# Routing the last three batches through one expert a token, in a two-layer attention and mixture kernel

## The reference, cut to what matters

```python
probs = softmax(xt @ Wg)                       # 2048 tokens, 8 experts
sel   = top_k(probs.T, 256)                    # each expert picks 256 tokens
tok2exp = argmax over the experts that picked it, else over all
weights = probs[token, tok2exp]
for e in range(8):
    gate = where(tok2exp == e, weights, 0)
    out += gate * (gelu(xt @ W1[e]) @ W2[e])   # W1: 128x256, W2: 256x128
x = x + gb * out
```

## Time and profile before

| | us |
|---|---|
| median of 3 runs | 757.88 (756.86 to 758.79) |
| the profiled execution's span | 758.0 |
| PE busy | 738.9 (97%) |
| DVE busy | 550.8 (73%) |
| ACT busy | 383.1 (51%) |
| POOL busy | 187.3 (25%) |

### The profile page before, as it was taken

How to read it: one execution, slowest core, us unless ns; L and a number is a source line. 1 busy time by engine, 2 the same in 40 slices (tenths; PEclk the granted TensorE clock), 3 DMA queues, 4 the chain that set the end, 5 groups by cost and what they waited for, 6 DMA issues and landing times.

```text
span 758.0 us, 16817 instructions
## 1 busy us (share of the span) xinstructions
PE 738.9 (97%) x6559; PEld 558.0 (74%) x6559; DVE 550.8 (73%) x1642; ACT 383.1 (51%) x1063; POOL 187.3 (25%) x235
## 2 busy tenths in 40 slices
PE   7899999999999999999999999999999899999996
PEld 5666757775786578657865776688578778999996
DVE  4877785868867886778677867787959664255997
ACT  3755656355545654564456445643561446554422
POOL 0232522154015402530253025304210422000000
PEclk9999999999999999999999999999999999999999
DMA  7950020402040204020302130113204304000000
GB/s 229 397 120 1 29 57 2 112 1 57 8 106 2 57 19 96 2 56 20 96 2 55 28 87 18 41 39 76 57 2 113 112 3 111 1 1 1 16 21 22
DMA packets 55702, 43.07 MB, mean 57 GB/s; under 512 B 37900, under 2 KB 48804, under 8 KB 54216
## 3 DMA queue, kind: packets, MB, share of 16 engines
q1 hardware_dynamic: 55624, 42.01, 20.7%
HBM read 32.42 MB, written 9.58 MB: 55 GB/s over the span
## 4 chain that ended last, share of the span: by engine, by line
PE 85%; DVE 9%; ACT 2%; DMA 1%; issue 1%; POOL 1%; SPq 0%; DVEq 0%; ACTq 0%
PE ps L1755 15%; PE ps L1838 14%; PE ps L1898 8%; PE ps L2061 4%; PE ps L2039 4%; PE ps L1741 4%; PE ps L2008 4%; PE ps L1763 4%; PE ps L1850 3%; PE ps L1789 3%; PE ps L1776 3%; DVE shared L1484 2%; DVE shared L1477 2%; PE ps L1705 2%; PE ps L1921 2%; PE ps L1933 2%
## 5 line engine op out<-in xcount | busy, mean ns | idle before, releaser
L1755 PE MATMUL ps<-veF,hB 128*128 128x512 f32 x256 | 121.5, 606 | 0.0
L1303 DVE COPY_PREDICATED shared<-ghot,ps 128x512 f32<-128x512 int32 x128 | 88.2, 726 | 3.4 <-PE ps L1755 0.6
L850 ACT ACTIVATE sc<-sc,nmax 128x128 f32<-128x128 f32 (+1 forms) x128 | 57.2, 447 | 58.3 <-DVE nmax L1289 58.3
L1755 PEld LDWEIGHTS ps<-veF,hB 128*128 128x128 f32 x256 | 45.2, 189 | 49.4 <-issue 40.5
L650 POOL TENSOR_TENSOR sc<-sc,rg 128x384 f32<-128x384 f32 x64 | 51.6, 827 | 70.0 <-DVE rg L1276 70.0
L707 POOL TENSOR_TENSOR ve<-mv,eps 128x2 f32<-128x2 f32 x24 | 8.6, 357 | 229.9 <-DVE mv L1189 229.9
L1838 PE MATMUL ps<-early_masks,oeF 128*128 128x256 f32 x256 | 62.9, 385 | 0.0
L1838 PE MATMUL ps<-wide,oeF 128*128 128x256 f32 x256 | 62.3, 386 | 0.0
L1898 PE MATMUL ps<-hC,early 128*64 128x128 f32 x1024 | 61.7, 275 | 0.1
L2039 PE MATMUL ps<-hE,veF 128*128 128x256 f32 x256 | 59.5, 382 | 0.3 <-ACT wide L959 0.3
L1898 PEld LDWEIGHTS ps<-hC,early 128*64 128x64 f32 x1024 | 55.6, 137 | 5.3 <-issue 3.4
(11 more groups left out here) (253 smaller groups left out, 1529.5 us busy)
## 6 DMA issues: line engine op xcount, KB each, us to landing
chosen<-hot_scratch SPq DMA_DIRECT2D x16, 512.0 KB, 5.8
v_scratch<-shared SPq DMA_DIRECT2D x16, 512.0 KB, 5.2
vg<-v_scratch SPq DMA_DIRECT2D x16, 512.0 KB, 5.4
veF<-in_L_ffn_value_experts SPq DMA_DIRECT2D x1, 2048.0 KB, 9.3
oeF<-in_L_ffn_output_experts SPq DMA_DIRECT2D x1, 2048.0 KB, 14.2
early<-in_L_attn_w_qkv SPq DMA_DIRECT2D x1, 1536.0 KB, 14.9
shared<-bias_scratch SPq DMA_DIRECT2D x2, 512.0 KB, 5.8
veF<-in_L_ffn_W SPq DMA_DIRECT2D x1, 1024.0 KB, 5.2
```

Source lines behind the costliest of these rows:

```text
L850: act.activation(v, v, ACT.Exp, bias=nmax[:, h % RING, t:t + 1], scale=-1.0, accum_out=denB[:, h * T + t:h * T + t + 1]).then_inc(s_("f_e" ...
L1303: dve.copy_predicated(val[:, t, :].rearrange("p (h k) -> p h k", h=HF), ghot[:, t * HF:(t + 1) * HF, e].bitcast(I32).unsqueeze(2) .broadca ...
L1755: pe.matmul(ps[:, vbank(j), :], tok(hB, t), veF[:, :].rearrange("p (h e k) -> p e h k", h=HF, e=EF)[:, e, :, :], start=True, stop=True).th ...
```

## The change

Batches 0 to 4 stay dense (`DENSE = 5`). The 768 tokens of batches 5 to 7 (six tiles) are sorted by expert. Each expert's tokens fill whole tiles of 128 places, the rest of its last tile is padding, so 13 tiles (`PLACES = 6 + 8 - 1`) hold any split of them. A row has 386 numbers: the token's features, its x, its gate, its weight and its number.

- GpSimd prepares constants and the x, gate, number and weight parts of the rows; TensorE turns the features of the six tiles back in slots of batches 2 and 3, and ScalarE copies them into the rows. SP fills the scratch of 13 x 128 rows in DRAM with padding.
- VectorE chooses first for the six sorted tiles, then for the ten dense ones. TensorE counts with seven small matmuls in slot 28 of batch 4 how many tokens of the same expert stand ahead of each. VectorE works out each token's place and each tile's expert.
- GpSimd writes the rows to their places with six indirect DMAs, SP reads them back in five loads, GpSimd copies the W1 of each tile's expert to a fixed place (13 register loads, 13 copies of 128x256).
- TensorE does eight filling matmuls, loads 13 registers, and then in 17 steps transposes tile j, multiplies tile j-2 with its W1 and tile j-4 with its W2, with ScalarE's copy and GELU between.
- VectorE does the kept batches 0 to 3, sorted tiles 0 to 3, kept batch 4, sorted tiles 4 to 12. A sorted tile is two operations: output times weight times gate, and the sum with x. GpSimd stores each finished tile to its tokens' rows of the output with an indirect DMA; numbers beyond the last token (padding) are dropped.
- `direct_one`, `last_tile` and the dense work of batches 5 to 7 on TensorE and ScalarE are gone. Old semaphores are used a second time under new names (`since` adds the count reached before).

```diff
+DENSE = KEPT
+SORTED_B = B - DENSE
+SORTED_T = SORTED_B * T
+FIRST_T = DENSE * T
+PLACES = SORTED_T + E1 - 1
...
+LOADS = ((0, 1), (1, 2), (2, 5), (5, 10), (10, 13))
+FILL = 8
+TURNED_BACK = {(2, 2 * E1 + 6): (0, 2), (3, 2 * E1 + 6): (2, 3)}
+COUNTED_AT = (4, 28)
+WEIGHED = ()
...
+            since(sp, "t_ones", 4)
+            sp.dma_start(sorted_dram.rearrange("(j p) c -> p j c", p=P),
+                         padding.unsqueeze(1).broadcast_to([P, PLACES, ROW])).then_inc(s_("t_padded"), 16)
+
+            sp.wait_ge(s_("t_sorted"), 16 * SORTED_T)
+            for i, (lo, hi) in enumerate(LOADS):
+                sp.dma_start(rows_of(lo, hi), sorted_dram.rearrange("(j p) c -> p j c", p=P)[:, lo:hi, :]
+                             ).then_inc(s_("t_rows%d" % i), 16)
...
+            for i in range(SORTED_B):
+                b = DENSE + i
+                pool.tensor_copy(staged(i)[:, :, ID_AT].bitcast(I32), token_no[:, i * T:(i + 1) * T]).then_inc(s_("t_staged"), 1)
+                pool.tensor_copy(staged(i)[:, :, D:2 * D], x[:, b * T:(b + 1) * T, :]).then_inc(s_("t_staged"), 1)
+                pool.tensor_copy(staged(i)[:, :, 2 * D:3 * D],
+                                 gate1[:, b, :].unsqueeze(1).broadcast_to([P, T, D])).then_inc(s_("t_staged"), 1)
...
+            since(pool, "t_staged", 4 * SORTED_B)
+            since(pool, "t_h", SORTED_B)
+            since(pool, "t_padded", 16)
+            since(pool, "t_place", 1)
+            for i in range(SORTED_T):
+                pool.indirect_dma_start(sorted_dram, bass.IndirectOffsetOnAxis(ap=token_place[:, i:i + 1], axis=0),
+                                        staged(i // T)[:, i % T, :], None).then_inc(s_("t_sorted"), 16)
+
+            since(pool, "t_expert", 1)
+            for j in range(PLACES):
+                e = pool.value_load(expert_of[0:1, j:j + 1], min_val=0, max_val=E1 - 1)
+                pool.tensor_copy(row_w1(j), w1[:, bass.ds(e, 1), :].rearrange("p e f -> p (e f)")).then_inc(s_("t_w1"), 1)
+
+            rows_out = out.rearrange("b n d -> (b n) d")
+            for i, (lo, hi) in enumerate(LOADS):
+                since(pool, "t_rows%d" % i, 16)
+                for j in range(lo, hi):
+                    since(pool, "t_done", j + 1)
+                    pool.indirect_dma_start(rows_out, bass.IndirectOffsetOnAxis(ap=row(j)[:, ID_AT:ID_AT + 1].bitcast(I32), axis=0),
+                                            row(j)[:, 0:D], None, bounds_check=TOK - 1,
+                                            oob_is_err=False).then_inc(s_("t_stored"), 16)
...
+                        since(act, "t_turned", n + 1)
+                        for i in range(lo, hi):
+                            act.activation(staged(i)[:, :, 0:D],
+                                           ps[:, 3, (i - lo) * N:(i - lo + 1) * N].rearrange("p (t d) -> p t d", d=D),
+                                           ACT.Copy).then_inc(s_("t_h"), 1)
...
+            for step in range(PLACES + 2):
+                if step < PLACES:
+                    since(act, "t_rowT", step + 1)
+                    if step >= 4:
+                        since(act, "t_hid", step - 3)
+                    act.activation(turned_row[step % 4], turned_row_at(step), ACT.Copy).then_inc(s_("t_hs"), 1)
+                if step >= 2:
+                    j = step - 2
+                    since(act, "t_hid", j + 1)
+                    if j >= 4:
+                        since(act, "t_y", j - 3)
+                    act.activation(row_gelu[j % 4], hidden_row_at(j), ACT.Gelu).then_inc(s_("t_g"), 1)
...
+            rank, best, _, _ = choose(FIRST_T, TILES)
+            since(dve, "t_ones", 10)
+            dve.tensor_tensor(hot[:, 0:SORTED_T, :], rank, best, ALU.is_equal).then_inc(s_("t_hot"), 1)
+
+            rank, best, chosen_one, top = choose(0, FIRST_T)
+            link(dve.tensor_tensor(chosen_one, rank, best, ALU.is_equal))
+            dve.tensor_tensor(weight[:, 0:FIRST_T, :], chosen_one, top, ALU.mult).then_inc(s_("t_weight"), 1)
+
+            c = s_("t_chain")
+            since(dve, "t_pre", 1)
+            dve.tensor_tensor(over128, ps[:, 0, 48:56].unsqueeze(2).broadcast_to([P, E1, SORTED_T]),
+                              steps128.unsqueeze(1).broadcast_to([P, E1, SORTED_T]), ALU.is_gt).then_inc(c, 1)
+            since(dve, "t_chain", 1)
+            dve.tensor_reduce(tiles_e, over128, AX.X, ALU.add).then_inc(c, 1)
...
+            dve.tensor_scalar(token_place, place_f, 1.0, None, ALU.mult).then_inc(s_("t_place"), 1)
...
+            dve.tensor_scalar(expert_of, expert_f, -1.0, None, ALU.add).then_inc(s_("t_expert"), 1)
...
+            def then(ins):
+                k[0] += 1
+                ins.then_inc(s_("e_k"), 1)
+                dve.wait_ge(s_("e_k"), k[0])
...
+            def sorted_one(j):
+                since(dve, "t_y", j + 1)
+                for i, (lo, _) in enumerate(LOADS):
+                    if lo == j:
+                        since(dve, "t_rows%d" % i, 16)
+                r = row(j)
+                then(dve.scalar_tensor_tensor(out=r[:, 2 * D:3 * D], in0=output_row_at(j), scalar=r[:, W_AT:W_AT + 1],
+                                              in1=r[:, 2 * D:3 * D], op0=ALU.mult, op1=ALU.mult))
+                dve.tensor_tensor(r[:, 0:D], r[:, D:2 * D], r[:, 2 * D:3 * D], ALU.add).then_inc(s_("t_done"), 1)
+
+            for b in range(DENSE - 1):
+                kept_one(b)
+            for j in range(PLACES):
+                if j == 4:
+                    kept_one(DENSE - 1)
+                sorted_one(j)
...
+                for t in range(lo * T, hi * T):
+                    mm = pe.transpose(ps[:, 3, (t - lo * T) * P:(t - lo * T + 1) * P],
+                                      hE[:, (FIRST_T + t) * P:(FIRST_T + t + 1) * P], ident[:, :])
+                mm.then_inc(s_("t_turned"), 1)
...
+                since(pe, "t_hot", 1)
+                pe.matmul(ps[:, 0, 0:56], rm[:, 2, :], hot[:, :, :].rearrange("p t e -> p (t e)"), start=True, stop=False)
+                for t in range(SORTED_T):
+                    n = SORTED_T - t
+                    mm = pe.matmul(ps[:, 0, (t + 1) * E1:56].rearrange("p (t e) -> p t e", e=E1), ones[:, :],
+                                   hot[:, t, :].unsqueeze(1).broadcast_to([P, n, E1]), start=False, stop=(n == 1))
+                mm.then_inc(s_("t_pre"), 1)
...
-            for b in range(1, B):
+            for b in range(1, DENSE):
...
+            for _ in range(FILL):
+                pe.matmul(ps[:, 1, :], ident[:, :], wide[:, 4, :], start=True, stop=True)
+
+            since(pe, "t_expert", 1)
+            expert = [pe.value_load(expert_of[0:1, j:j + 1], min_val=0, max_val=E1 - 1) for j in range(PLACES)]
+            since(pe, "t_place", 1)
+            for step in range(PLACES + 4):
+                if step < PLACES:
+                    j = step
+                    for i, (lo, _) in enumerate(LOADS):
+                        if lo == j:
+                            since(pe, "t_rows%d" % i, 16)
+                    if j >= 2:
+                        since(pe, "t_hs", j - 1)
+                    pe.transpose(turned_row_at(j), row(j)[:, 0:D], ident[:, :]).then_inc(s_("t_rowT"), 1)
+                if 0 <= step - 2 < PLACES:
+                    j = step - 2
+                    since(pe, "t_hs", j + 1)
+                    since(pe, "t_w1", j + 1)
+                    if j >= 3:
+                        since(pe, "t_g", j - 2)
+                    if j == 2:
+                        pe.wait_ge(s_("y_free"), DENSE * 4 + 1)
+                    for g in range(2):
+                        mm = pe.matmul(hidden_row_at(j)[:, g * P:(g + 1) * P],
+                                       row_w1(j)[:, g * P:(g + 1) * P],
+                                       turned_row[j % 4], start=True, stop=True)
+                    mm.then_inc(s_("t_hid"), 1)
+                if step >= 4:
+                    j = step - 4
+                    since(pe, "t_g", j + 1)
+                    if j >= 3:
+                        since(pe, "t_done", j - 2)
+                    for g in range(2):
+                        mm = pe.matmul(output_row_at(j), row_gelu[j % 4][:, g * P:(g + 1) * P],
+                                       w2[:, bass.ds(expert[j], 1), g, :].rearrange("p e d -> p (e d)"),
+                                       start=(g == 0), stop=(g == 1))
+                    mm.then_inc(s_("t_y"), 1)
```

More of the change, by code:

```diff
@@ new lines, in _ @@
+            since(pool, "t_best", 1)
+            for i in range(SORTED_B):
+                pool.tensor_copy(staged(i)[:, :, W_AT], kmax[:, FIRST_T + i * T:FIRST_T + (i + 1) * T]
+                                 ).then_inc(s_("t_staged"), 1)
+            since(pool, "t_staged", 4 * SORTED_B)
[5 more added lines that the diff above has]
+                                        staged(i // T)[:, i % T, :], None).then_inc(s_("t_sorted"), 16)
@@ new lines, in route @@
```

(25 more changed lines are left out.)

227 lines of the change are left out of this document (145 added, 82 removed).

## The result

| | before | after |
|---|---|---|
| median, us (9 runs each, taken together) | 758.43 (756.57 to 759.38) | 760.84 (758.41 to 761.76) |
| after / before | | 1.0033, 95% interval 1.0021 to 1.0045 |
| span of the profiled execution | 758.0 | 758.5 |

The changed kernel is slower by 2.5 us, 1.6 to 3.4. Its profiled execution took 760.3 by the clock of the runs, 1.8 more than its span of 758.5; the 1.8 is there in every run of it (1.76 to 1.85), and in the kernel before too (1.75 to 2.04).

A forecast was written before the change was run, and what follows sets the result against it. TensorE and VectorE were both taken as full, VectorE's chain setting the gain. Tile 4 done at 749.6, plus 9.4 for nine stores and 2.0 landing, gave 761.0; with TensorE's clock (761.9), 761.5 was taken, range 754 to 769.

The forecast's parts named there:

- nine stores: GpSimd's indirect stores left behind tile 4: 9 x 1.04 = 9.4 us, from 749.6 to 759.0.
- the lock: Two-operand VectorE and SBUF-reading GpSimd instructions exclude each other; thirteen W1 copies hold VectorE 0.40 each, 5.2 us.
- kept batches start: VectorE starts its kept batches at 712.4 instead of 705.12, after choice, count and small operations: 7.3 us given back.
- kept batches 0 to 3 and the copies: On VectorE from 712.4: 22.6 us for the batches plus 5.2 for GpSimd's copies, to 740.2.
- landing: The last indirect store lands 2.0 us after GpSimd's stores end at 759.0, giving 761.0.
- the clock: TensorE at 1.2 GHz after idling under kept batch 4: last store landed 761.9 instead of 761.0; 761.5 taken between.
- the prediction's own sign: Kept batches 0 to 3 on VectorE last about 28 us together; if 22.6, the lock's step is wrong.
- The row that was to show the other direction: VectorE's four products begun at 149.41, during GpSimd's work, took 2.60 us; read as VectorE waiting for GpSimd.
- The indirect DMA: On GpSimd, no row shows one; taken at 1.04 us like a 128x512 product, with ends 0.5 and 2.0.
- The scatter: GpSimd's six indirect DMAs into the scratch, 6 x 1.04 from 711.7 to 717.9, landed at 719.9.
- the cover of 8 to 13 us: Slack between TensorE's first output at 727 and VectorE asking for it at 735 to 740.
- Rival 4: Late scatter or landing makes VectorE wait for the first output; decides after 740, 765 to 775 us; chance 0.07.

The follow-up runs named there:

- fixed_copies: Changed kernel with its thirteen W1 copies taking a fixed expert's W1, without register loads: 760.06 us, one execution.
- weighs_four: Changed kernel with ScalarE multiplying in the weights of kept batches 1 to 4, kept batch 4 ahead of tile 0: 756.52 us, 0.9974 of the kernel before.

## Why the prediction was right, and where its numbers were not

The forecast was 761.5 and slower by 0.5%; measured were 760.84 and 0.33%. What was named as the end is the end: VectorE gets back less than TensorE, GpSimd is the last engine, and its nine stores behind tile 4 close the span. That the number came within 0.7 us is luck, in two places.

In the sum, the lock was priced 4 us too high and the stores about 2 too low. With the lock at its measured 1.2 and all else as written, the sum is 757.5, which the prediction itself calls no change: that it said slower hangs on an error.

In the baseline, the sum took the execution's own time to be its span, which leaves out 1.8 us. But the execution that it started from was 1 to 2 us longer than the usual one, and that nearly makes up for it. As a span, 761.5 was 3.0 above the traced execution and 2.5 above the median. By its steps, in spans:

| step | predicted | measured | effect, us |
|---|---|---|---|
| kept batches start | 712.4 | 711.08 | -1.3 |
| kept batches 0 to 3 and the copies | 27.8 | 23.57 | -4.2 |
| tiles 0 to 3 | 3.0 | 3.33 | +0.3 |
| kept batch 4, tile 4 | 6.4 | 6.24 | -0.2 |
| from tile 4 to the start of its store | 0 | 0.79 | +0.8 |
| nine stores | 9.4 | 11.30 | +1.9 |
| landing | 2.0 | 2.2 | +0.2 |

These make 761.0 into 758.5; the last 0.5 of the forecast was for the clock.

The start: 1.1 of the 1.3 us are the lead that this execution had already at 577 us, so the choice and the count were priced well. The weights were there at 706.11, not 707.7; the wait for the count was the longer for it, 2.50 instead of 1.8, and the eleven small operations took 2.47.

The price of the lock is the largest error, and by the prediction's own sign (22.6 or 28 us for kept batches 0 to 3) this step failed: they took 23.57. It was taken as each copy's whole length, 0.40, laid on VectorE. The two engines do exclude each other, but VectorE, with 0.02 us between operations, is almost never the one that waits: it lost 1.2 us to thirteen copies and GpSimd 7.5 (12.7 less 13 x 0.40). The row that was to show the other direction did not carry it: VectorE's four products took 2.60 us, 0.08 more than 4 x 0.63, although GpSimd worked 0.25 us into them.

The Trainium skill (SBUF — State Buffer, Summary: rules for kernel authors) says that of a VectorE instruction with two SBUF inputs and a GpSimd one that reads SBUF, the second to issue blocks until the first has finished. The stores agree (they end 0.85 to 0.87 us after the product). The runs show in addition that the one with the dense queue pays little: 0.09 us a copy, 0.14 at most.

The indirect DMA was taken at 1.04, by the row of a 128x512 product. It is busy 0.98, which is close, but the next one begins 0.30 later, and the step left that out: 1.29 each, 2.3 over nine. Had the lock cost VectorE what was written, the end would have been 4 us later, 762.5 as a span.

The scatter is the step that came nearest to turning the forecast over. It was to take 6.2 us and took 10.9: 1.4 by the gaps between the DMAs, 3.3 since VectorE's products held GpSimd up. The lock had been weighed for the copies and not for the DMAs in front of them. TensorE's first steps took 7.75 us from the first sorted row to the first output, not 5, 2.55 of them the wait for row 2, which had been given no time of its own. So the first output came at 734.3 and not at 727, and the cover of 8 to 13 us shrank to 0.4. Rival 4 (VectorE waits for the first output) was one small step from holding, as ScalarE's weighing and the run without copies show; its point of decision was put at 740 because the lock was overpriced.

The Trainium skill (SBUF — State Buffer, Who interferes with whom) tells that descriptor generation for GpSimd's DMAs was not seen to be stalled by `tensor_tensor`, which has no 2-port mode. Here it is: 3.06, 1.40 and 1.90 us beside two-operand products, 0.96 to 1.25 with VectorE idle, and 3.07 for a store. These DMAs take their 128 offsets from SBUF; whether it is that read that waits was not tried. The Trainium skill's fixed cost of about 2.0 us for a DMA issued by GpSimd (DMA: Bandwidth & Descriptors, Anatomy of one DMA — SWDGE (gpsimd) path) stands beside 2.2 here, counted from the end of GpSimd's instruction to the landing.

TensorE's half clock was seen (0.50, 0.71), made its output late (VectorE waited 1.25 us at 747.64), and behind tile 4 cost nothing, since GpSimd had tiles in hand: 761.5 should have stayed at 761.0. That preparations, the padding store and the register loads are hidden held. Two slips in the working reach no number that counts: all loads at the rate of the 2 MB load are 11.4 us, not 11.7, and without the lock tile 4 starts at 743.6, not 743.8.

## What to carry to other kernels

When work is taken from the engine that is full and handed to others, add up the last queue instruction by instruction, with the gap between two: thirteen stores of 1.29 us on one queue are 17 us, and when they follow without a pause only the start of the first is left to win. A chain of small instructions beside a dense stream of two-operand VectorE work pays the lock itself, and it pays most at the first ones, which is where the latency of the whole chain is made. Of two engines that exclude each other, charge the wait to the one with gaps in its queue. And before a traced execution serves as the base of a sum, see where it stands among the others.

## What the runs showed of the hardware that was not expected

- An indirect DMA of 128 rows takes GpSimd 0.96 to 1.00 us whether a row has 512 or 1544 bytes (the first of a series up to 1.25), with 0.30 to the next, and a store lands 2.2 later. Beside VectorE's products with two operands in SBUF it takes up to 3.09 (fixed_copies) and ends 0.85 to 0.87 after the product.
- A register load in front of a copy on GpSimd shows as 46 ns and cost nothing that shows in thirteen.
- ScalarE multiplies a 128x128 tile with a weight for each partition every 0.294 us (64 in 18.79; each lasts 0.385 to 0.393 and they overlap), and neither VectorE nor GpSimd at work beside it lengthened it (weighs_four).
- The time outside the span grew from 1.8 to medians of 2.1 to 2.5 us in the three kernels with eighteen fillers.
